# A recommendation tower on one core: ids and constants reordered at the start, transposes and early matmuls moved, last layers in halves

## The reference

```python
e = jnp.stack([tbl_f[ids[:, f]] for f in range(39)], axis=1)      # 512 x 39 x 32
p, q = e[:, ROW, :], e[:, COL, :]                                  # 741 pairs
z = jnp.einsum('bpc,apc,bpa->bp', p, w, q)                         # 512 x 741
h = jnp.concatenate([z, dense_ctx], axis=1)                        # 512 x 757
h = jnp.maximum(h @ W_top1 + b_top1, 0.0)                          # 512 x 512
h = jnp.maximum(h @ W_top2 + b_top2, 0.0)                          # 512 x 256
return h @ W_top3                                                  # 512 x 1
```

## Time and profile before

| | |
|---|---|
| median of 3 runs | 207.26 us (206.95 to 208.34) |
| profiled execution, its time | 205.15 us |
| profiled execution, its span (first to last instruction) | 203.4 us |
| mean granted TensorE clock | 0.983 |
| PE busy | 186.7 us (92%) |
| DVE busy | 142.3 us (70%) |
| POOL busy | 134.7 us (66%) |
| ACT busy | 41.8 us (21%) |

### The profile page before, as it was taken

The page is one execution under the profiler, slowest core; times in us unless marked ns, Lnnn a source line. Parts: engine busy times, 40 slices in busy tenths (PEclk is TensorE's granted clock), DMA queues, the critical chain, the costliest instruction groups (busy, mean ns, idle before and its releaser), DMA issues.

```text
span 203.4 us, 3185 instructions
## 1 busy us (share of the span) xinstructions
PE 186.7 (92%) x1284; PEld 60.2 (30%) x1284; DVE 142.3 (70%) x132; ACT 41.8 (21%) x55; POOL 134.7 (66%) x202
## 2 busy tenths in 40 slices
PE   6999979979999999999089999999989996999895
PEld 3434533322223222232032223322322221222340
DVE  4499999946989898996404489899883339764500
ACT  4887940030002001101011120101111121111413
POOL 8899999988888989898989898985012220423000
PEclk9999999999999999999958999999999999999999
DMA  5999940000000000000000000010000000000000
GB/s 147 272 281 414 389 125 16 10 13 13 11 13 14 15 10 13 14 13 10 12 12 11 16 11 14 10 16 12 0 2 3 0 0 0 0 5 0 0 0 0
DMA packets 6681, 9.75 MB, mean 48 GB/s; under 512 B 1973, under 2 KB 4469, under 8 KB 6666
## 3 DMA queue, kind: packets, MB, share of 16 engines
q1 hardware_dynamic: 3722, 8.03, 12.3%
q0 software_dynamic: 2944, 1.51, 4.6%
HBM read 9.53 MB, written 0.00 MB: 47 GB/s over the span
## 4 chain that ended last, share of the span: by engine, by line
PE 47%; POOL 42%; issue 5%; DMA 2%; ACT 1%; DVE 1%; DVEq 0%
POOL gathered L386 32%; PE ps L581 16%; PE ps L594 14%; POOL pause L393 10%; PE ps L605 10%; PE ps L618 3%; PE ps L613 2%; PE ps L559 1%; DMA gathered<-tbl,ids_sb 1%; DMA ids_sb<-ids 1%; PE ps L624 1%; DVE prod L492 1%; ACT eT L432 1%; ACT z_sb L435 0%; ACT prod L457 0%
## 5 line engine op out<-in xcount | busy, mean ns | idle before, releaser
L492 DVE TENSOR_TENSOR prod<-ps,eT 128x1024 f32<-128x1024 f32 (+2 forms) x91 | 109.8, 1264 | 40.6 <-PE ps L581 32.1
L386 POOL DMA_INDIRECT gathered<-tbl,ids_sb x92 | 93.0, 1010 | 15.3 <-issue 15.0
L581 PE MATMUL ps<-eT,w_sb 32*128 32x512 f32 (+2 forms) x380 | 69.5, 639 | 3.5 <-DVE prod L492 1.9
L594 PE MATMUL ps<-prod,sel 128*32 128x512 f32 x380 | 52.1, 610 | 0.0
L581 PEld LDWEIGHTS ps<-eT,w_sb 32*128 32x128 f32 (+2 forms) x380 | 21.9, 183 | 50.4 <-issue 32.7
L400 POOL TENSOR_TENSOR tabs<-tabs 128x512 f32<-128x512 f32 x8 | 10.1, 1266 | 36.6 <-ACT tabs L449 36.6
L477 DVE TENSOR_SCALAR hot<-ids_half,row_of 125x2048 bf16<-125x2048 f16 x34 | 28.1, 893 | 4.1 <-ACT ids_half L414 4.1
L393 POOL MEMSET pause<- 128x256 f32 x91 | 29.9, 328 | 0.1
L605 PE MATMUL ps<-z_sb,w_sb 128*128 128x512 f32 x40 | 22.1, 669 | 1.4 <-ACT eT L432 1.4
L548 PE MATMUL ps<-hot,lower 125*32 125x512 bf16 x272 | 21.6, 394 | 0.0
L594 PEld LDWEIGHTS ps<-prod,sel 128*32 128x32 f32 x380 | 8.0, 108 | 35.1 <-issue 20.7
(11 more groups left out here) (33 smaller groups left out, 51.5 us busy)
## 6 DMA issues: line engine op xcount, KB each, us to landing
w_sb<-w SPq DMA_DIRECT2D x1, 1536.0 KB
gathered<-tbl,ids_sb POOLq DMA_INDIRECT x92, 2.4
tabs<-hot SPq DMA_DIRECT2D x3, 448.0 KB
w_sb<-wst SPq DMA_DIRECT2D x1, 640.0 KB, 13.0
w_sb<-wst SPq DMA_DIRECT2D x1, 576.0 KB
tabs<-hot SPq DMA_DIRECT2D x1, 560.0 KB
w_sb<-wst SPq DMA_DIRECT2D x1, 512.0 KB, 10.5
w_sb<-w SPq DMA_DIRECT2D x1, 512.0 KB
```

The source lines that it names most:

```text
L386: pool.indirect_dma_start(gathered[J][:, b, K * r:K * r + K], None, tables[f], bass.IndirectOffsetOnAxis(ap=ids_sb[:, F * b + f:F * b + f ...
L492: dve.tensor_tensor(prod[:, x:x + n, :], ps[:, s:s + n, :], eT[:, I:I + 1, :].broadcast_to([P, n, B]), ALU.mult).then_inc(multiplied, 1)
L581: mm = pe.matmul(ps[:, RUN_BANK[p] + i - first, :], w_sb[rows, w_tile(q), :], eT[rows, J, :], start=True, stop=True)
L594: mm = pe.matmul(z_ps[K * (u % G):K * (u % G) + K, :], sel[:, u // G, :], prod[:, RUN_SLOT[p] + t - FIRST_TILE[p], :], start=(u < G), stop ...
```

## The change

It has four parts.

- **Start.** The first ids for the lookups (`hot_ids`) are loaded by a DMA that ACT issues, no longer behind `ids` on SP. POOL makes the identity first, and `sel` after the row numbers; DVE makes `spread` as soon as the identity is there, and PE waits for `sel` only at the first sums. The four matmuls that spread the first block's ids count one by one; ACT copies the first two and the fourth, DVE the third.
- **Order.** KEEP_LEAD becomes 1 for blocks 6, 7 and 8 (3 for the rest), PACE becomes 1, and the rule `near` goes.
- **Last layers.** The last `z` block is copied in two halves of 256 samples. Layers 1 and 2 are done half by half, with as many columns in all and twice as many matmuls. Layer 3 is done in quarters of 128 samples, which land on partitions 0, 32, 64 and 96.
- **Output.** One DMA of four rows of 128 numbers takes the place of one row of 512.

```diff
-KEEP_LEAD = 3
-PACE = 2
+KEEP_LEAD = {J: 1 if J in (6, 7, 8) else 3 for J in GATHERED}
+PACE = 1
...
-        near = any(0 < FIRST_QUAD[T] - KEEP_LEAD - q <= 1 for T in GATHERED)
-        if early and since >= PACE and not near and all(there(zb) for zb in ROUNDS[early[0][1]]):
+        if early and since >= PACE and all(there(zb) for zb in ROUNDS[early[0][1]]):
...
+        h1_ps = [[ps[:, bank, of] for bank in banks] for of, banks in zip(HALVES, [(1, 5, 2, 3), (0, 4, 7, 6)])]
+        h2_ps = [[ps[:, bank, of] for bank in banks] for of, banks in zip(HALVES, [(1, 5), (2, 3)])]
...
-            sp.dma_start(hot_ids_sb[:, :], hot_ids).then_inc(hot_ids_in, 16)
...
+            pool.wait_ge(consts_zero, 1)
+            pool.affine_select(out=ident[:, :], in_=ident[:, :], compare_op=ALU.not_equal, fill=1.0, base=0,
+                               pattern=[[-1, P]], channel_multiplier=1).then_inc(consts_made, 1)
...
+            act.dma_start(hot_ids_sb[:, :], hot_ids).then_inc(hot_ids_in, 16)
...
+                        for part in (slice(0, 2), slice(3, 4)):
+                            act.wait_ge(ids_spread, part.stop)
+                            act.activation(ids_half[h][0:HP, part, :], ids_ps[h][:, part, :],
+                                           ACT.Copy).then_inc(ids_half_made, 1)
...
+            dve.wait_ge(ids_spread, 3)
+            dve.tensor_copy(ids_half[0][0:HP, 2, :], ids_ps[0][:, 2, :]).then_inc(third_made, 1)
...
+            for i, of in enumerate(HALVES):
+                for k in range(M1):
+                    pe.wait_ge(h1_kept, M1 * i + k + 1)
+                    if k == 0:
+                        pe.wait_ge(h1_added, M1 * (i + 1))
+                    for m in range(M2):
+                        mm = pe.matmul(h2_ps[i][m], w2_sb[:, k, P * m:P * m + P], h1_sb[k][:, of],
+                                       start=(k == 0), stop=(k == M1 - 1))
+                        if k == M1 - 1:
+                            mm.then_inc(h2_made, 1)
+            for i, of in enumerate(HALVES):
+                for k in range(M2):
+                    pe.wait_ge(h2_kept, M2 * i + k + 1)
+                    for c in range(2):
+                        g = 2 * i + c
+                        mm = pe.matmul(ps[K * g:K * g + 1, 4 * i, 0:P], w3_sb[:, k:k + 1],
+                                       h2_sb[k][:, P * g:P * g + P], start=(k == 0), stop=(k == M2 - 1))
+                mm.then_inc(y_made, 1)
```

More of the change, by code:

```diff
@@ L207, in turns, with halves_of @@
     return TURNS.index(J) + 1
+def halves_of(h):
+    return h + 2
 def lay_out_weights(w, W_top1):
@@ L434, in _ @@
                     act.wait_ge(summed, step[2])
-                    act.activation(z_sb[:, step[1], :], z_ps, ACT.Copy).then_inc(z_kept, 1)
+                    if step[1] < NZ - 1:
+                        act.activation(z_sb[:, step[1], :], z_ps, ACT.Copy).then_inc(z_kept, 1)
+                    else:
+                        for of in HALVES:
+                            act.activation(z_sb[:, step[1], of], z_ps[:, of], ACT.Copy).then_inc(z_kept, 1)
                 elif step[0] == "early":
@@ L493, in _ @@
                                           eT[:, I:I + 1, :].broadcast_to([P, n, B]), ALU.mult).then_inc(multiplied, 1)
-            for m in range(M1):
-                dve.wait_ge(h1_made, m + 1)
-                if m == 0:
-                    dve.wait_ge(early_kept, len(EARLY))
-                    dve.wait_ge(early_added, M1 * (len(ROUNDS) - 1))
-                    dve.wait_ge(summed, len(SUMS))
-                dve.tensor_tensor(h1_sum[m], h1_ps[m], h_early[0][:, m, :], ALU.add).then_inc(h1_added, 1)
+            for i, of in enumerate(HALVES):
+                for m in range(M1):
+                    dve.wait_ge(h1_made, M1 * i + m + 1)
+                    if i == 0 and m == 0:
+                        dve.wait_ge(early_kept, len(EARLY))
+                        dve.wait_ge(early_added, M1 * (len(ROUNDS) - 1))
+                        dve.wait_ge(summed, len(SUMS))
+                    dve.tensor_tensor(h1_sum[m][:, of], h1_ps[i][m], h_early[0][:, m, of],
+                                      ALU.add).then_inc(h1_added, 1)
         @block.tensor
@@ L622, in _ @@
-            for k in range(M2):
-                pe.wait_ge(h2_kept, k + 1)
-                mm = pe.matmul(y_ps, w3_sb[:, k:k + 1], h2_sb[k], start=(k == 0), stop=(k == M2 - 1))
-            mm.then_inc(y_made, 1)
+            for i, of in enumerate(HALVES):
+                for m in range(M1):
+                    if m == 0:
+                        pe.wait_ge(z_kept, NZ + i)
+                    if i == 0 and m == 0:
+                        wait_z(pe, NZ - 1)
+                        pe.wait_ge(multiplied, NRUN)
+                        side_free()
+                    pe.matmul(h1_ps[i][m], w1_sb[:, NZ - 1, P * m:P * m + P], z_sb[:, NZ - 1, of],
+                              start=True, stop=True).then_inc(h1_made, 1)
```

78 lines of the change are left out of this document (35 added, 43 removed).

## The result

The changed kernel took 199.25 us (median of 4 runs, 198.34 to 201.34), the kernel before 207.1 us beside it (4 runs, 205.09 to 208.34). The ratio is 0.964, interval 0.953 to 0.974: faster. (Medians are of all runs; ratios and intervals leave out runs over 1.5% above the fastest of the same kernel.) The profiled execution took 198.71 us, with a span of 197.0, and the one before took 205.15. So 6.44 us went between the two profiled executions where 7.4 was forecast.

What follows compares the result with a forecast made beforehand. Bound: POOL's gathers up to 99 us (42% of the chain), then PE (47%). Sums ending 6.6 us earlier plus 0.8 from the last layers make 7.4; 207.26 - 7.4 = 199.9 us, range 198.3 to 203.0.

Steps and rivals of the forecast that it cites:

- The walk: Step-by-step sum of PE's times through the kernel: 7.4 us less, so a profiled execution of 197.7 us.
- Block 7: PE reaches its transposes at 106.1, after the rows land at 101.5; the 4.96 wait and the slow clock go.
- Block 8: PE and the gathers meet at its transposes near 124.6; with the start's gain, PE waits 1.2 to 1.5 us.
- I take +0.2: Delay of the gathers from the new start, in us, between bounds of -0.96 and +1.19.
- The start worth nothing: PE's gain at the start all goes into the wait for block 8, so it gives nothing at the end.
- I take 1.2: PE's gain in us from the new start, between 0.6 and 1.7.
- Block 9: Transposes at 144.65 instead of 150.70 with rows there, quad 48 at 163.1, last sums ending 6.6 us earlier.
- Last layers: Halves and quarters at the kernel's end give 0.8 us, between 0.2 and 1.2.
- The gathers start earlier: Rival, 0.20: first gather shrinks by 0.96, POOL's constants are not held, 1.1 gained over the forecast, 198.8 us.
- The clock falls in the new wait: Rival, 0.10: the clock halves behind PE's wait of 1.2 to 2.0 for block 8, losing 2.9: 202.8 us.
- DVE's pace: Rival, 0.10: early steps in a row leave more quads bare at DVE's pace, costing 1.8: 201.7 us.
- The weight load comes out: Rival, 0.03: loads of 0.19 behind halved matmuls of layers 1 and 2 are exposed, adding 9.1: 209.0 us.

Runs made afterwards that it cites:

- second chip: The chip where the changed kernel was timed again with no edit: 201.77 us, ratio 0.976, against 207.0 us for the kernel before.
- second and third sets: Follow-up runs on two further chips, where the kernel before took 207.0 and 208.01 us.
- last layers alone: The kernel before with only the new last layers and the output of four rows: 253.5 us, ratio 0.987.
- block 8 early: The changed kernel with only block 8's KEEP_LEAD back at 3: 206.96 us, ratio 1.002.
- early steps kept: The changed kernel with one early step held until quad 46 and one more put behind quad 47: 199.86 us, ratio 0.956.
- all but the start: The changed kernel with the start of the kernel before: 255.59 us, ratio 1.015, in the first set; 201.79 us, ratio 0.977, when run again.
- order alone: The kernel before with only the new order: 258.49 us, ratio 1.012, in the first set; 201.95 us, ratio 0.975, when run again.
- `sel` by DVE: The changed kernel with `sel` made by DVE instead of POOL: 199.93 us, ratio 0.965.
- short pauses: The changed kernel with pauses of 64 instead of 256 columns between the gathers: 199.01 us, ratio 0.966.
- start alone: The kernel before with only the changed start: 254.64 us, no ratio on record.
- first set: Four follow-up runs of parts of the change on a chip where the kernel before took 255.05 us.

## Why the prediction was right and where it was off

**The size.** 199.9 was forecast and 199.25 measured, inside the range. On the second chip it was 201.77, inside as well. The walk itself, from one profiled execution to the other, gave 197.7 against 198.71, so it was 1.0 too good; the step that hid it is "the median, which lies 2.1 above the profiled time". After the change the median lies 0.5 above. The two errors cancel, so that the forecast came within 0.7 is partly luck. The runs of the kernel before have a clock between 0.959 and 0.983 in the second and third sets, those of the changed kernel mostly 0.983 to 1.000. That fits with a loss that the old order has in most executions and the new one in fewer, such as the 1.6 us behind the single wait of 1.95, seen with the last layers alone. But the runs of the kernel before were not taken apart, so the part of the clock in the 2.1 stays open.

**Block 7: right.** Transposes without a wait at 105.61 (106.1 forecast), quad 28 at 107.19 (107.6; the terms add up to 107.7), full clock. The 0.4 is the start's gain at PE, which I had counted only at block 8.

**Block 8: the mechanism was right, two terms were off, and one was missing.** A wait of 1.2 to 1.5 was forecast at 124.8; it was 1.34 at 125.77. Terms: "the last gather ... lands 2.23 later" was 2.56, and "I take +0.2" for the gathers was +0.81 (123.17 against 122.36). The first gather ended 0.21 later, as taken. What I left out is what the faster lookups do to POOL: DVE's comparisons begin 1.7 us earlier and so meet the pause at 6.55 (+0.44) and the gather at 7.48 (+0.26). At about 80 us the gathers stand at 79.93 against 79.10, and at 100.12 against 99.29: between these two executions nothing is added later. 0.6 of issue and 0.33 of landing make the 1.0 by which the sum failed. The Trainium skill, "SBUF — State Buffer", section "Who interferes with whom", gives the exclusive lock by which both would happen, and the rows agree: a selection of 0.45 took 1.28 beside `spread`, and a pause of 0.33 took 0.77 beside a comparison. They don't show when an instruction is held: the pauses at 8.68 and 10.38 took 0.33 beside comparisons too. The missing term is the scatter of the gathers. The third one is issued at 7.47 to 7.54 with the new start and at 6.82 with the old, in every trace where POOL makes `sel` and the pauses are full. But by block 8 this is buried: the last gather is issued at 123.17, 125.19, 126.10 and 125.51 with the new start (the change twice, block 8 early, early steps kept), and at 122.36, 125.76 and 124.41 with the old (before, all but the start, order alone). That is 3.7 us from first to last, over three chips, against the 0.2 that I took.

**The start worth nothing: right** as far as the runs can tell, at 201.77 with it and 201.79 without. Its size at PE was off: "I take 1.2" was 0.52 at the first transposes (43.03 against 43.55). DVE's first comparison did move to 6.32 (6.4 forecast) and PE's first lookup from 9.95 to 8.87; half of this went away, as PE's matmuls came to the double pace at about the same time as before, between 12.5 and 12.8 us, and were slow until then.

**Block 9: right.** From quad 36 to its transposes 18.27 (18.25 forecast), waits of 0.92 (1.0 forecast) and 1.95, and from quad 48 to the last sums 15.65 (15.59). Blocks 8 and 9 end 1.0 late only because quad 36 starts at 127.35 instead of 126.4.

**Last layers: right in size, not in its parts.** 0.83 in all against 0.8; 0.79 of it within the span in the changed kernel, and 0.8 in the kernel that has this part alone. I had 0.2 for each of four pieces. Layer 3 alone gave 0.86 (1.88 before, 1.02 now, both by the timeline), the first copy 0.17, and the piece behind layer 3 took 0.2 back. That the sum held is luck.

**The rivals.** *The gathers start earlier* fell: they start later. Its price was tried with `sel` by DVE, and there block 8 was earlier by 0.64 and the end was not, because of the clock in block 9. *The clock falls in the new wait* did not come true in the two profiles of the changed kernel (waits of 1.34 and 1.10 left it at 1.00), but it is not refuted: with the early steps kept, whose order is the same up to there, the wait was 3.71 and the clock fell. It came true at another place as well, behind the waits in block 9. I had taken them as harmless because the single 1.95 of one profile had been; in another execution of the old order it was not. That the clock held in the profile of the changed kernel is luck, and the waits were priced as idling only. *DVE's pace* fell: PE reached block 8's transposes 17.24 behind quad 28 (125.77 - 1.34 - 107.19) where my walk had 16.95, so it cost 0.3 and not 1.8. *The weight load comes out* fell: layer 2's records take 0.216 each. The groups by form (us busy, mean ns of one) show as long a load as before, and twice as many:

```profile
L654 PEld LDWEIGHTS ps<-prod,w_sb 128*128 128x128 f32 x32 | 6.1, 190 | 0.8
```

In this rival the prediction also told only a part of the Trainium skill, "TensorE: Matmul & The Clock Gate", section "The mechanism". The section has the rule that it told, and another sentence that lets a load go ahead of running matmuls when its row group does not conflict *or when it goes to the background weight buffer*. By the second case the loads stay hidden, and the rows agree with it: 0.216 per record, with loads of 0.190.

## What to carry to other kernels

Moving a step that waits behind work that is ready anyway pays twice where the wait also lowers the clock: 4.96 us of idling at block 7 and some 3 us of half clock behind it. The bound then moves to the next block of the same stream, so look at that one's arrival on both sides before placing it: here one number, block 8's lead, decided between a ratio of 1.00 and one of 0.96 to 0.98. Take the scatter of the arrival from more than one execution: one profile showed a wait of 1.34, another one of 3.71 at the same place. And don't call a wait harmless because one profile shows full clock behind it: the 1.95 before quad 48 cost its idling in some executions and 1.6 us more in others, and work put into it and into the 0.92 ahead of it took 2.04 away and left the clock full in both profiles.

## What the runs showed of the hardware

- Granted clock behind waits of PE: 0.50 behind 3.71, 4.96 and 6.43 us; 1.00 behind 0.60, 0.90, 1.10 and 1.34. Behind 0.92 and 1.95 with 2.1 us of work between, 1.00 in four profiles (the changed kernel twice, all but the start and order alone in the later sets) and 0.50 to 0.6 for some 2 us in five (`sel` by DVE, short pauses, block 8 early, and order alone and all but the start in the first set). Behind a single 1.95, 1.00 in two (before, start alone) and 0.50 in one (last layers alone). What decides between these was not found.
- The lookup matmuls reach their double pace at 11.6 to 18.7 us in the profiles of the later sets (the earliest with `sel` by DVE, the latest with order alone and all but the start) and at about 21.9 us with all but the start in the first set, and the granted clock column is 1.00 on both sides of that step. Between two executions of the changed kernel it made 2.5 us at the first transposes (43.03 and 45.52). What sets the moment was not tried.
- Layer 3's quarters land on different groups of 32 partitions, and 16 matmul records of 128 columns take 1.02 us, against 1.88 for the same columns in 4 records of 512. At the 0.216 of 256 columns they would take 1.7 one after another (an estimate), so they overlap. That the groups are the reason was not tried.
- On the chip of the first set, PE and DVE stalled for 2 to 5 us at a time as long as indirect gathers ran, while POOL's gathers kept their 0.95 us, and the kernel before took 255 us instead of 207. No run told why.
